# Splitting eight batches between two expert groups: 7 + 1 in place of 6 + 2

## The reference

```python
logits = xf @ Wr.T + expert_bias
rw = softmax(logits); topw, topi = top_k(rw, 2); topw = softmax(topw)
shared = swiglu(xf, sW1, sW2, sW3)
h  = silu(einsum('td,efd->etf', xf, eW1)) * einsum('td,efd->etf', xf, eW3)
eo = einsum('etf,edf->etd', h, eW2)
out = X + shared + einsum('te,etd->td', combine, eo)   # 2 of 8 experts per token
```

## Time and profile before

| | us |
|---|---|
| median of 3 runs | 2292.13 |
| lowest, highest | 2290.48, 2292.91 |
| the profiled execution, its own time | 2309.25 |
| its span | 2307.5 |
| mean granted TensorE clock | 0.931 |
| busy over the span: TensorE, VectorE, ScalarE, GpSimd | 1978.6, 1403.0, 1193.6, 702.0 |

### The profile page before, as it was taken

How to read it: one execution, slowest core, us unless ns; L and a number is a source line. 1 busy time by engine, 2 the same in 40 slices (tenths; PEclk the granted TensorE clock), 3 DMA queues, 4 the chain that set the end, 5 groups by cost and what they waited for, 6 DMA issues and landing times. The chain is left out here.

```text
span 2307.5 us, 37967 instructions
## 1 busy us (share of the span) xinstructions
PE 1978.6 (86%) x13464; PEld 1002.5 (43%) x13464; DVE 1403.0 (61%) x3126; ACT 1193.6 (52%) x2157; POOL 702.0 (30%) x693
## 2 busy tenths in 40 slices
PE   4899999999999999967999999983988898679972
PEld 2556565655565556542233222321333333246641
DVE  5664656564656565526778676765478876544344
ACT  2554545454545454534777666771456664335531
POOL 2110201110111110122333223303457765532266
PEclk8999999999999999987899888995899999799997
DMA  5111111111111011113122232201001110133355
GB/s 155 46 38 38 38 38 37 37 38 38 37 28 44 22 40 36 37 50 58 42 49 55 51 56 56 47 1 45 1 10 42 60 53 22 46 94 124 105 160 155
DMA packets 97081, 122.82 MB, mean 53 GB/s; under 512 B 14304, under 2 KB 73984, under 8 KB 96896
## 3 DMA queue, kind: packets, MB, share of 16 engines
q1 hardware_dynamic: 79872, 93.11, 17.1%
q0 software_dynamic: 6144, 16.79, 2.3%
q10 hardware_dynamic: 10880, 10.49, 1.4%
HBM read 52.64 MB, written 33.82 MB: 37 GB/s over the span
## 5 line engine op out<-in xcount | busy, mean ns | idle before, releaser
L1104 DVE TENSOR_REDUCE x_NM<-x_pm 128x1 f32<-128x512 f32 x512 | 343.5, 688 | 127.2 <-PE x_pm L847 125.1
L1029 ACT ACTIVATE x_PR<-x_pS 128x512 f32<-128x512 f32 x512 | 300.9, 601 | 136.4 <-PE x_pS L863 130.8
L376 PE MATMUL a_pa<-a_PR,a_V 128*128 128x512 f32 (+3 forms) x1024 | 341.8, 441 | 0.7 <-ACT a_PR L456 0.3
L456 ACT ACTIVATE a_PR<-a_pS 128x384 f32<-128x384 f32 (+1 forms) x384 | 201.4, 525 | 207.2 <-PE a_pS L365 204.9
L538 DVE CUSTOM_DVE_ANT_0 a_pm<-a_pm,a_causal 128x128 f32<-128x128 f32 (+3 forms) x512 | 247.2, 509 | 83.8 <-PE a_pm L351 69.0
L611 POOL CAST a_YT_hi<-a_Y 128x512 f16<-128x512 f32 x64 | 40.2, 628 | 760.3 <-DVE a_Y L546 760.3
L847 PE MATMUL x_pm<-x_KT,x_QT 48*128 48x512 f16 x512 | 208.9, 427 | 23.0 <-DMA x_QT<-q_k_parts 22.3
L863 PE MATMUL x_pS<-x_QT,x_KT 49*128 49x512 f16 x512 | 204.4, 416 | 15.4 <-ACT x_PR L1029 14.3
L546 DVE TENSOR_TENSOR a_Y<-a_pa,a_RS 64x512 f32<-64x512 f32 x128 | 88.0, 688 | 182.4 <-ACT a_RS L464 181.3
L376 PEld LDWEIGHTS a_pa<-a_PR,a_V 128*128 128x128 f32 x1024 | 174.8, 192 | 29.7 <-ACT a_PR L456 11.3
L351 PE MATMUL a_pm<-a_KA,a_QA 128*128 128x128 f16 (+3 forms) x512 | 142.5, 308 | 43.7 <-DVE a_NM L538 27.9
(11 more groups left out here) (361 smaller groups left out, 4506.2 us busy)
## 6 DMA issues: line engine op xcount, KB each, us to landing
a_QA<-a_nat_q SPq DMA_DIRECT2D x128, 128.0 KB, 2.3
m_xr<-sent SPq DMA_DIRECT2D x80, 128.0 KB
made<-e_eo ACTq DMA_DIRECT2D x40, 256.0 KB
a_KA<-a_nat_k SPq DMA_DIRECT2D x64, 128.0 KB, 2.3
a_KB<-a_nat_k SPq DMA_DIRECT2D x64, 128.0 KB, 2.4
x_KT<-q_k_parts SPq DMA_DIRECT2D x48, 128.0 KB, 4.3
x_QT<-q_k_parts SPq DMA_DIRECT2D x48, 128.0 KB, 4.3
m_xr<-in_w SPq DMA_DIRECT2D x12, 512.0 KB
```

The costliest lines, as they stand in the source:

```text
L376: m = eng.matmul(pa[j % 2][:, P * kc:T], V[:, u % 2, kc, j, :], PR[:, i % 4, at:at + T - P * kc], start=(kc == 0), stop=(kc == TT - 1))
L456: eng.activation(PR[:, i % 4, 0:n], pS[i % 2][:, 0:n], ACT.Exp, scale=SCALE).then_inc(s_e, 1)
L1029: eng.activation(PR[:, kc, j, :], pS[i % 2][:, :], ACT.Exp, scale=SCALE).then_inc(s_e, 1)
L1104: eng.tensor_reduce(NM[:, v % 2, c:c + 1], ring_bank("max", v, n)[:, :], AX.X, ALU.max, negate=True).then_inc(s_red, 1)
```

## The change

```diff
@@ -1476,7 +1476,7 @@
 def moe_block(nc, keep, mem, k, x_res, out_dram, d, B):
     NE = 9
     ER = NE - 1
-    n2 = max(1, B // 4)
+    n2 = max(1, B // 8)
     groups = [Group(nc, 0, 0, B - n2, ER), Group(nc, 1, B - n2, n2, ER)]
```

## The result

The changed kernel took 2326.81 us (median of 4 runs, 2324.50 to 2339.52), the kernel before beside it 2291.31 us (4 runs, 2277.97 to 2292.91): ratio 1.0179, 95% interval 1.0126 to 1.0232, slower by 35 us. The forecast was 2320, +27.8. Measured again in a later session, with eight runs of the changed kernel and 28 of the one before, the same pair gave 2305.84 against 2284.19 us, ratio 1.0085 [1.0055, 1.0115], +21.7 us. The direction is the same, the size is not, and the forecast lies between the two.

What follows compares the result with a forecast made beforehand. In the experts TensorE bounds until 2200 us, then GpSimd to the end. Part 3's +13.7 and +14.1 for Parts 1 and 2 (20.5 - 6.4) sum to +27.8 on 2292.13: 2319.9, taken as 2320, range 2303 to 2329.

Steps and rivals of the forecast that it cites:

- Part 3: Hand-over from attention to the experts: group 0's table and loads come late, so the experts start 13.7 us later.
- The lower bound, -3.6: Bound of Part 3: all table steps straight behind batch 6's ranks, SyncE's end at 2031.3, -3.6 us.
- Part 1: First gather in the experts: it waits for pair 31 in place of 27, 4 x 5.12 = +20.5 us.
- Part 2: GpSimd from first to last gather: fewer subtractions, one wait gone, 94.26 - 6.4 = 87.9 us; VectorE's added wait zero.
- enough cover for the last store: In Part 2: fourteen gathers (17.9 us), not eight, precede the second group's first gather, so the 1.40 us wait goes.
- interlock: Rival, chance 0.11: gather landings slow, VectorE's additions hold the next pair back, +7.5 us on top, 2327.4.
- Room on GpSimd: Rival, chance 0.04: seven gathers a pair hide beside TensorE, only trailing gathers count, -10.2 us; hand-over hidden too, 2278.3.
- Hand-over hidden: Rival, chance 0.19: the planner puts the table right behind batch 6's ranks, Part 3 is -3.6 to +2, say 2304.

Runs made afterwards that it cites:

- block kernel: Changed kernel with the first group's 23 table steps directly behind its last token's ranks on VectorE: 2291.67 us, ratio 1.0041 to the kernel before.

## Why the forecast was right in direction and wrong in size

**Part 3, the hand-over: right, shown.** The forecast order of VectorE's steps came out to the step: seven ahead of O(7,0), sixteen behind O(7,1). FT(7,1)'s copy is at 1988.46 + 16.7 = 2005.2 (forecast 2004.1, before 2014.14). The table's L1423 ends at 2028.1 (2026.6). The experts start 13.3 us later by the first pair of profiles and 12.8 by the second, for +13.7. The block kernel shows that this is the table's lateness: with it mended 12.5 us are back. The lower bound, -3.6, was wrong: a table directly behind the ranks holds up the last batch's routing as before, and gives +0.4.

**Part 1, four pairs: right in mechanism, 2 us too dear.** 20.5 us were forecast; 18.4 and 17.9 measured. The four pairs are there (the stores lie 5.1 us apart as before), but the last store of the first group landed 2.3 us sooner; the instruction packet that fell on it in the kernel before no longer did, which is the likely cause and was not tested. I had read 6.39 us of idle in the earlier trace rows as the price of the wait; 2.3 of it did not carry over.

**Part 2, GpSimd's work after the first gather: the step that failed.** The forecast was 94.26 - 6.4 = 87.9 us, with zero for VectorE's wait and "enough cover for the last store". In the execution that the result stands on it was 97.57, +3.3 over before: 9.7 us over the forecast. About 5.3 us of it is GpSimd waiting for H_hi, and 6.0 us more than the normal gap for the last store; about 1.6 us goes the other way. The interlock that I had priced as a rival is the smaller part: 1.7 us of the H_hi waits, where the forecast had zero and as its bound +7.5, and with its condition removed nothing is gained when signals are on time. The larger part, 3.6 us of H_hi and the 6.0 us, stands behind completion signals of TensorE that came up to 10.7 us behind its rows in that session, and the changed kernel has them on its path: seven gathers a pair leave VectorE's chain 0.8 us of slack by the forecast's own count, and the fourteen gathers cover 19.5 us behind the last subtraction (2283.56 to 2301.56 + 1.22 + 0.30), where the last store then needed 25.5. Where the signals are on time, it took 86.3 us twice: my 87.9, less 0.025 us a gather. What "enough cover" left out is a delay that the profile of before already showed, in ScalarE's waits for "remote", and that the forecast did not use.

Sums. First pair: 13.3 + 18.4 + 3.3 + 0.1 = +35.1 for the forecast's 13.7 + 20.5 - 6.4 = +27.8. Second pair: 12.8 + 17.9 - 9.4 = +21.3, in which the kernel before had 1.5 us more between its gathers than in its first profile (one idle of 2.82 us behind a late landing). That the forecast lies between the two sessions is no merit of it: it had neither the late signals, which added, nor the sooner landing, which took away. The two sessions differ by 14 us, the medians likewise (+35.5, +21.7), and of this 12.7 us lie in the step from first to last gather. The changed kernel's two sets of runs do not overlap (2324.5 and up, 2315.8 and down), so it belongs to the session and is no scatter. That late signals made these 12.7 us is read from the traces of two sessions; no run brought them about. What delays them was not found: packets of the DMA queues took the same time in both sessions (software queue 150 to 161 ns on average), and the granted clock over 2220 to 2300 was 0.70 and 0.71.

**The rivals.** Room on GpSimd did not happen: a gather cost 1.25 to 1.28 us everywhere. Hand-over hidden did not happen in the changed kernel; forced by the block it gives +5.8 us by medians, +9.5 by profiles, near the +10.5 that this rival had. The interlock did not decide here, yet with three gathers a pair it is the largest effect of this study, 40.8 us.

## What to carry to other kernels

A number that splits work into groups also sets ratios that other constants were tuned to. Before it is moved, write down what each count must be a multiple of: here gathers a pair against gathers a semaphore cost 40.8 us at three to four, under 1 at seven to four with signals on time, nothing that can be told at four to four. The opposite move of the one made here, with that ratio mended, gained 15 us: the long serial work of one engine began earlier and fitted beside the engine that bounds, which is about half of the gain by the profiles, and the attention was shorter, which is the other half.

Compare stages from their own first row, and profile the changed kernel twice before explaining a stall: the waits that I first put down to the change were gone in the next session.

## What the runs showed of the hardware that was not expected

TensorE's completion signals can come late, by its rows: in one session's two profiles, in the last stage's attention (a wait of 2.54 us for the usual 0.90) and beside the gathers (up to 10.7 us behind the rows, where ScalarE otherwise starts 0.03 us behind them); in the twelve later profiles no wait of any engine ends with "remote". Why is open. A 256 KB store on which a 16 KB instruction packet fell landed in 4.4 us for 2.1, in both profiles of the kernel before at the same place; that the packet is the cause is inferred from its place between the store's packets, and no run moved it alone.
